# A two-layer conditional convolution, attention, FFN and Fourier stack on one core: input loaded ahead of two parameter packs, the taps of a strip in three steps, and a new order of steps

## The reference

```
x = conv(x, L0);  x = conv(x, L1)          # two conditionally mixed inverted bottlenecks
t = tokens(x)
t = t + linear_attention(ln(t))            # no softmax: (q k^T) v
t = t + quantised_ffn(ln(t))               # fp8e5 products, fp16 sums
t = t + fourier_mixer(ln(t))               # 1x1, fft over 3136 tokens, complex scale, relu, ifft, 1x1
t = t + quantised_ffn(ln(t))

conv: rw = sigmoid(mean(x) @ Wr + br)      # a router per image mixes 4 experts' weights
      h  = relu(bn(x @ Wk(rw)))            # 24 -> 96 channels
      h  = relu(bn(depthwise3x3(h, rw)))   # 9 taps per channel
      x  = bn(h @ Wk2(rw)) + x             # 96 -> 24
```

## Time and profile before

| | |
|---|---|
| median of 3 runs | 2447.91 us (2443.51 to 2450.33) |
| profiled execution | 2448.76 us, span 2447.0 us, mean granted TensorE clock 0.903 of full speed |
| busy | PE 85%, PEld 50%, DVE 79%, ACT 65%, POOL 5% |
| matmuls | 19720, of which 4608 are the taps of line 757 (404.5 us busy) |
| instructions | 48861 |

### The profile page before, as it was taken

The page is one execution under the profiler, slowest core; times in us unless marked ns, Lnnn a source line. Parts: engine busy times, 40 slices in busy tenths (PEclk is TensorE's granted clock), DMA queues, the critical chain, the costliest instruction groups (busy, mean ns, idle before and its releaser), DMA issues.

```text
span 2447.0 us, 48861 instructions
## 1 busy us (share of the span) xinstructions
PE 2087.6 (85%) x19720; PEld 1234.5 (50%) x19720; DVE 1924.6 (79%) x3745; ACT 1583.8 (65%) x2704; POOL 114.6 (5%) x290
## 2 busy tenths in 40 slices
PE   3777988999979989999789987898889998887865
PEld 2233433664446634665347634376347644663753
DVE  4986988799949999699959996698978999366253
ACT  3344447775777677765777666776767667767544
POOL 0000000000000000000000000000000000000000
PEclk9887989999979999999989997899999999987765
DMA  5001000100020000100020002000010000000000
GB/s 147 1 1 21 1 1 5 18 2 1 1 40 2 2 1 15 28 2 1 1 40 2 2 1 41 1 2 1 1 32 2 2 1 1 22 2 1 21 1 20
DMA packets 108591, 29.62 MB, mean 12 GB/s; under 512 B 104144, under 2 KB 104272, under 8 KB 107984
## 3 DMA queue, kind: packets, MB, share of 16 engines
q1 hardware_dynamic: 108368, 26.50, 5.3%
HBM read 16.85 MB, written 9.63 MB: 11 GB/s over the span
## 4 chain that ended last, share of the span: by engine, by line
DVE 40%; PE 36%; ACT 13%; issue 7%; SPq 3%; DMA 1%; ACTq 0%; DVEq 0%
DVE acc L1505 19%; PE P L757 7%; PE P L738 5%; PE P L972 4%; DVE SQ L1670 3%; PE P L1064 3%; SPq L598 3%; DVE arena L1654 3%; PE P L909 2%; DVE arena L1670 2%; PE P L779 2%; DVE roots L1670 2%; PE P L806 2%; PE P L985 2%; DVE T L1521 1%
## 5 line engine op out<-in xcount | busy, mean ns | idle before, releaser
L1505 DVE SCALAR_TENSOR_TENSOR acc<-H,Dm,acc 128x784 f32<-128x784 f32 x1024 | 999.2, 1029 | 30.7 <-ACT acc L1140 30.3
L738 PE MATMUL P<-T,Wk 112*128 112x448 f32 (+1 forms) x768 | 385.7, 593 | 55.7 <-ACT H L1133 32.2
L757 PE MATMUL P<-H,diag 64*64 64x392 f32 x4608 | 404.5, 501 | 15.5 <-DVE T L1521 12.4
L1133 ACT ACTIVATE H<-P,biasA 128x448 f32<-128x448 f32 (+1 forms) x384 | 237.3, 622 | 206.0 <-PE P L738 182.7
L757 PEld LDWEIGHTS P<-H,diag 64*64 64x64 f32 x4608 | 174.9, 135 | 228.7 <-issue 191.1
L738 PEld LDWEIGHTS P<-T,Wk 112*128 112x128 f32 x768 | 130.8, 200 | 172.2 <-ACT H L1133 104.1
L1163 ACT ACTIVATE acc<-P,biasT 128x392 f32<-128x392 f32 x128 | 71.7, 584 | 128.8 <-PE P L757 128.8
L1140 ACT ACTIVATE acc<-H,Dm 128x784 f32<-128x784 f32 x128 | 121.6, 950 | 8.1 <-PE P L779 5.8
L1169 ACT ACTIVATE acc<-acc,biasA 128x784 f32<-128x784 f32 x128 | 118.4, 948 | 10.7 <-DVE acc L1505 10.4
L997 PE MATMUL P<-pack_b,arena 128*96 128x112 f32 x928 | 112.3, 268 | 10.6 <-DVE roots L1670 4.6
L972 PEld LDWEIGHTS P<-pack_b,arena 113*64 113x64 f32 x1792 | 112.7, 216 | 16.8 <-issue 7.6
(11 more groups left out here) (209 smaller groups left out, 3630.0 us busy)
## 6 DMA issues: line engine op xcount, KB each, us to landing
xin<-in_x SPq DMA_DIRECT2D x224, 42.0 KB, 2.3
out_y<-arena SPq DMA_DIRECT2D x8, 1176.0 KB, 6.1
pack_b<-in_pack_b SPq DMA_DIRECT2D x1, 3870.5 KB, 17.5
arena<-in_pack_s SPq DMA_DIRECT2D x1, 1584.0 KB, 8.6
pack_a<-in_pack_a SPq DMA_DIRECT2D x1, 1084.0 KB, 5.3
pack_i<-in_pack_i SPq DMA_DIRECT2D x1, 320.0 KB, 3.2
arena<-in_pack_k SPq DMA_DIRECT2D x1, 192.0 KB, 3.4
```

The source lines that it names most:

```text
L738: pe.matmul(conv_rows(slice(0, 128), HB[(NP * s + e) % len(HB)], n), Wk1[:, 128 * j:128 * (j + 1)], image_rows(T[q % 3], a, n), start=True ...
L757: last = pe.matmul(conv_rows(slice(64 * h, 64 * (h + 1)), CVB + r, HH), diag[64 * r:64 * (r + 1), tap, :], H1[64 * r:64 * (r + 1), slot(s, ...
L1133: act.activation(H1[:, slot(s, j), o:o + n, 1:1 + HW], conv_rows(slice(0, 128), HB[(NP * s + e) % len(HB)], n), ACT.Relu, bias=biasA[:, j, ...
L1505: ins = ve.scalar_tensor_tensor(a, H1[:, slot(s, j), r:r + SR, c:c + HW], Dm[:, j, tap:tap + 1], a, ALU.mult, ALU.add)
```

## The change

Four edits:

- SyncE loads `a` after the first four input groups as before, then the last three groups of quad 0, and only then `s` and `b`.
- In `taps` there is a `yield` ahead of tap 3 and of tap 6, so that a strip's 36 matmuls are three steps of 12 and others can come between. TensorE's `d` stream has 320 steps in place of 192.
- GpSimd waits for its own second small memset (`ones_ready`) before it copies the terms of the middle's second layer norm.
- All of `TURNS` is new. Two lines of it are shown.

```diff
 TURNS = {
     "gpsimd": (
-        "d1 c9 m2 c3 b1 c2 m1 c6 b2 c2 m2 c4 b1 c1 m1 d1 c2 b3 m1 d1 c2 m1 c2 b1 c1 m1 c5 b1 c1 b2 c1 m1 c1 m1 "
+        "c2 b1 c7 m1 c2 m1 c4 m1 c3 d1 b1 c2 b1 c1 m1 d1 m1 c2 d1 c1 b1 c2 b1 m1 c4 b2 m1 c2 m1 c3 b1 m1 c1 d1 "
...
     "tensor": (
-        "c15 d1 c9 d1 c4 d3 c2 m1 c2 d4 c1 d3 c9 d1 c8 d3 m1 c1 d1 c1 d1 c3 m1 c2 m1 d2 c1 m1 d1 m1 d1 m3 d1 "
+        "c17 d2 c3 d2 c4 d2 c1 d1 c1 d1 c1 d1 c1 d1 c2 d2 c1 d1 c1 d2 c1 d5 c4 m1 c4 d3 c5 d1 c2 d1 c4 d3 m1 "
...
             load(0, range(XG))
-            for key in ("a", "s", "b"):
+            sp.dma_start(pack_t["a"], packs["a"]).then_inc(par_loaded["a"].sem, 16)
+            load(0, range(XG, NCK))
+            for key in ("s", "b"):
                 sp.dma_start(pack_t[key], packs[key]).then_inc(par_loaded[key].sem, 16)
             for q in range(NQ):
-                load(q, range(XG, NCK))
+                if q > 0:
+                    load(q, range(XG, NCK))
                 if q + 1 < NQ:
                     load(q + 1, range(XG))
...
                 pool_e.memset(bdw[2][:, 0:MR], 0.0).then_inc(ones_ready.sem, 1)
+                pool_e.wait_ge(ones_ready.sem, ones_ready.at(q, 2))
                 yield from shift_terms(q, normM, 1)
...
                 for tap in range(NTAP):
                     dy, dx = tap // 3, tap % 3
+                    if tap and dx == 0:
+                        yield
                     for r in range(2):
```

## The result

| | before | after |
|---|---|---|
| median | 2449.12 us (2443.51 to 2453.07, 4 runs) | 2392.96 us (2388.01 to 2397.24, 4 runs) |
| ratio | | 0.9772, 95% interval 0.9744 to 0.9799 |
| span of the profiled execution | 2447.0 us | 2386.2 us |
| mean granted TensorE clock in it | 0.903 | 0.922 |

The kernel became 56 us faster, 2.3%.

What follows compares the result with a forecast made beforehand. No engine was full: VectorE paces the start, TensorE and VectorE in turn the middle, dependent work the end. 2448.8 - 10.7 (start) + 4 (breaks) - 10.5 (order) = 2431.6, so 2431 us; range 2405 to 2451.

Steps and rivals of the forecast that it cites:

- The gain of 10.7: Quad 0's first layer: earlier input gains 8.0 us and fewer VectorE waits 2.7; bounds 5 and 12.5.
- The cost of a break: Taps on TensorE: about 0.2 us a break, 11 us over 55 breaks, 4 us on the chain (0 to 10).
- The step that failed: New order behind quad 0: 10.5 us gained, 1.5 in each of seven quads; bounds 40 gained and 25 lost.
- the direct gain is small: Breaks in the tap blocks: VectorE does not starve under a block, only ScalarE does, so breaks directly give little.
- The steady stretch: Between the routers of quads 2 and 7: shorter by some 7 us; over 20 shorter would mean the order gives much more.
- the first rival: Whole order: breaks let FFN matmuls go where ScalarE starves, 35 us in all, 2406 us; chance 0.22.
- which no break removes: ScalarE's rectification waits 128.8 us for the tap blocks' results; breaks were said not to remove this.
- the order gives much more: Whole order: FFN matmuls placed where ScalarE starves bring back 5 us a quad, 35 in all, 2406 us; chance 0.22.
- The reachable sum of idle time: Steady stretch, 430 to 2130 us: room for at most some 26 us in each of six quads, most of it dependence.
- Eaten where it arises: Quad 0's first layer: TensorE's clock falls during `setup_rest`, strips 2 and 3 run taps slowly; 4 us gained, 2448; chance 0.16.
- the 4.2 that the sum kept: End of quad 0's first layer: VectorE waits of 4.2 us stay, behind the last taps, rectification and projection.
- The broken strips hold the path: Tap strips: inserted pieces delay each strip's next step, 20 us lost plus the breaks' 4, 2461 us; chance 0.12.

Runs made afterwards that it cites:

- new_old_load: The changed kernel with the old load order, packs s and b ahead of input groups 4 to 6: 2406.54 us, 0.9829.
- start_only: The kernel before with the new load order and the middle's first step (`setup_rest`) moved as in the changed kernel, taps in one step: 2439.20 us, 0.9983.
- the two computed pairs: The changed kernel with step orders refitted by calculation, without and with breaks: first pair 2412.18 and 2403.17 us, second pair 2429.59 and 2410.68 us.
- old_breaks: The kernel before with new loading, `setup_rest` moved, GpSimd's new wait, taps in three steps and 47 breaks put in: 2503.64 us, 1.0232.
- join_first: The changed kernel with every strip's three tap steps set back to back at the place of the first: 2497.54 us, 1.0232.
- refit_nobreaks: The changed kernel without the yield in taps, its order on four engines refitted by calculation to whole strips: 2412.18 us, 0.9857.

## Why the prediction was wrong

**The start was right, with one wait a little long.** TensorE's wait for group 4 fell to 4.35 us, where under 4 was said. Group 6 was issued at 18.22, where 16.6 was forecast and up to 19 allowed: pack a did hold the issues up, by 1.6 us of the possible 2.4. The router's last copy ended at 31.5 (30.8 forecast), the first tap began at 36.4 (35.6), `setup_rest` took 12.1 us bare (12.7) with no wait for a pack, and the last addition ended at 118.8 (118 to 122 forecast, 119.1 by the sum). The gain of 10.7 was 11.1, and `new_old_load` prices the load order at 13.6 in the whole time (5 to 23 by the two intervals), `start_only` the whole start at 5.4. GpSimd's large memset, at 86.6 us, cost nothing that this layer's end shows.

**The cost of a break was about right.** From 48 blocks in 295.6 us to 88 pieces in 306.0 is 0.26 us a piece, where I had 0.2, so 14 us of TensorE against 11. With the share of the chain it is 5 us, against 4. No experiment prices it by itself. TensorE's busy time nevertheless fell by 17 us where up to 27 more was forecast, at a granted clock of 0.922 in place of 0.903: the sum had no term for the clock.

**The step that failed** is the term for the new order together with "the direct gain is small". Forecast: order 10.5 gained, breaks 4 lost, 6.5 net. Measured: 56 less the start's 5 to 14, so 42 to 51, beyond even the bound of 40 that I gave the order. The steady stretch became 30.4 us shorter, where 7 was forecast and over 20 was to mean the first rival. It failed in three places.

- The direct gain. I saw in six blocks that VectorE is busy under the taps and ScalarE is not the earlier trace rows; over all 48 blocks this holds (97% and 41%). From it I concluded that little can be gained since VectorE does not starve. But what is lost under a block is ScalarE's time. Its work then falls behind the block, and there it is what VectorE and TensorE wait for: VectorE's wait for ScalarE's part of the FFN is 86 us before, 59 after and 101 with all strips joined, and it doubles in quad 7's second layer when that is joined (4.0 to 8.8). The 128.8 us of ScalarE's wait for a block's result, "which no break removes", fell by 26.6 as well; its wait for hidden pieces (742 after), which was to fall, went from 182.7 to 190.6. TensorE's 26.4 us of idle time for the same ScalarE step stood in the earlier trace rows, and I did not weigh it. The rival "the order gives much more" named the mechanism, an FFN's matmul where ScalarE starves, with 35 us; in the two computed pairs the orders with breaks were 9 and 19 us ahead.
- The order. I priced it as what two orders of the same work share, 1.5 us a quad. The runs show that orders of the same steps scatter far more: 2403 and 2411 with breaks, 2412, 2430 and 2439 without, and 2498 to 2506 where one row is out of step. Nothing in the trace of before told which of these the new one would be. The reachable sum of idle time that I wrote down (26 us in each of six quads) was the better guide to the bound than the fifteenth of it that I took.
- The input behind quad 0. The sum has nothing for it: I wrote that only neighbours change behind quad 0. TensorE's idle time for its DMAs fell from 33 to 11 us and VectorE's wait ahead of the routers from 19 to 5. How much of it lies on the path isn't measured; the first layers, in which it falls, became 15 us shorter together.

The 46 us from `start_only` to the changed kernel split, by the first pair of computed orders, into 27 for a better order of whole strips, 9 for breaks on top and 10 by which the changed order is better than the computed one; by the second pair into 10, 19 and 18. These are differences of kernels that one method found, two of each kind; with 8 to 17 us between two of a kind, it is not a measured price of order and breaks.

**The rivals.** "Eaten where it arises" came in part: strips 2 and 3 did run their taps slowly (TensorE's timeline below; a full-speed piece of 24 takes 2.21 us), but VectorE's 18 taps covered strip 2, as the argument against had it, and strip 3 left 3.18 us bare in place of the 4.2 that the sum kept.

```profile
87.76 5.88 PE L763 MATMUL P<-H,diag 64*64 64x392 f32 x48 [2.67 <-DVE T L1527]
...
105.88 7.85 PE L763 MATMUL P<-H,diag 64*64 64x392 f32 x72 [3.17 <-DVE T L1527]
```

"The broken strips hold the path" is what `old_breaks` shows, 64 us where I had 24; in the changed kernel no such loss is left in the sum. A piece of 24 matmuls takes 2.21 us, and what follows begins 2.14 us after its start. By that the rule of the Trainium skill ("TensorE: Matmul & The Clock Gate", packing small matmuls), with which I had worked out 8 us on the path, is again not borne out at the end of a piece. A break also cost less in all than the 0.4 us that I had made of the rule: 0.26 by the recorded pieces, of which 0.17 are in the taps' own starts ((3 x 2.14 - 6.09) / 2).

**Open.** Whether an order without breaks exists that reaches 2393 wasn't shown or excluded. The changed order is ahead of the computed ones in quad 7's second layer, where their work stands otherwise; why was not tried. GpSimd's new wait and its new row were never taken alone, and neither was the earlier input behind quad 0.

## What to carry to other kernels

With engines that work off their queues in order, a long block on one engine can cost what the other engines cannot do in the meantime, also where the path's own engine lacks nothing: read the busy share of every engine under the block, and ask who waits for the idle one afterwards. Price a new order by the idle time that it could reach, with wide bounds on both sides; here orders of the same steps lay 110 us apart, most of a loss stayed in the layer where the rows did not fit, and such losses added up. Look at the waits for input in the steady stretch too: a new order moves the places where buffers come free. Never judge a part of a fitted order by taking it out alone: both halves of this change, put without the other, cost 64 to 113 us.

## What the runs showed of the hardware

- The granted clock and TensorE's busy time differ with the order. For the same 19720 matmuls the trace has 2070.6 us busy at a mean granted clock of 0.922 in the changed kernel, 2087.6 at 0.903 before, and 2105.4 at 0.895 in `join_first`. The 35 us between the first and the last can't be put down as 35 of the 107 us of span, since the chain goes through TensorE for only a third of it, and the link is loose: `old_breaks` has 2106.8 us at 0.902, `refit_nobreaks` 2070.7 at 0.913.
- Behind 1.1 MB of one pack two issues of input took 0.35 and 1.28 us more than the 0.49 of the others; behind 6.5 MB one took 10.7 more.
- An interruption of a block of small matmuls by other matmuls costs 0.26 us of TensorE's recorded time, as a mean of 40.
